# A four-layer graph network on one core: a second message tile and a looser wait in the message phase, and smaller constants

## The reference, cut to what matters

```python
edge_index = jnp.stack([src, dst])
x = x + gin(h, edge_index, ...)                       # two sums of x[src] by dst
x = x + attention(h, edge_attr3_2x32, src, dst, ...)  # below
x = x + tent(h, edge_attr_2, weight, edge_index)      # 4 x 4 tent basis
x = x + spline(h, edge_index, edge_attr_3, ...)       # STN, then a spline convolution

# attention, per edge (two heads of 32 features):
alpha = ee / jnp.maximum(denom[dst], 1e-09)
msg = jax.nn.softmax(en * r_feat * alpha, axis=-1)
g_agg = jax.ops.segment_sum(msg, dst, num_segments=n)

# spline_conv, second one of the STN (64 features in, 64 out):
z = jnp.einsum('ni,kio->nko', x, W).reshape(N * K, Fout)
gathered = z[col[:, None] * K + idx]          # 8 corners of the cell of the edge
msg = jnp.einsum('es,eso->eo', basis, gathered)
out = jax.ops.segment_sum(msg, row, num_segments=N)   # row = src
```

## Time and profile before

| | |
|---|---|
| median of 3 runs | 11980.05 us (11966.1 to 11993.72) |
| span of the profiled execution | 11729.7 us |
| its own time | not given apart from the span |
| TensorE busy, matmul / weight load | 6194.3 us (53%) / 4754.9 us (41%) |
| VectorE busy | 6868.2 us (59%) |
| ScalarE busy | 2989.3 us (25%) |
| GpSimd busy | 7301.5 us (62%) |
| bytes moved | 1760.69 MB, mean 150 GB/s |

### The profile page before, as it was taken

The page is one execution under the profiler, slowest core; times in us unless marked ns, Lnnn a source line. Parts: engine busy times, 40 slices in busy tenths (PEclk is TensorE's granted clock), DMA queues, the critical chain, the costliest instruction groups (busy, mean ns, idle before and its releaser), DMA issues. The chain is left out here.

```text
span 11729.7 us, 173426 instructions
## 1 busy us (share of the span) xinstructions
PE 6194.3 (53%) x40278; PEld 4754.9 (41%) x40279; DVE 6868.2 (59%) x17651; ACT 2989.3 (25%) x7270; POOL 7301.5 (62%) x10729
## 2 busy tenths in 40 slices
PE   4333244444688987666664555555544444662332
PEld 3222244434344443355553555555523333332222
DVE  6555666664322222577787666666656767655555
ACT  0000022221233332111112555555531111220000
POOL 3888788882366665577773333333327877228887
PEclk8555555555688987566665555555565555685555
DMA  6332222224455554222325777777621111587777
GB/s 195 113 113 57 62 62 62 63 62 131 149 190 187 193 186 134 52 74 74 78 77 147 281 285 278 280 284 281 235 81 43 44 41 43 178 323 219 221 222 199
DMA packets 894930, 1760.69 MB, mean 150 GB/s; under 512 B 487010, under 2 KB 487319, under 8 KB 889928
## 3 DMA queue, kind: packets, MB, share of 16 engines
q0 software_dynamic: 317952, 1023.05, 28.3%
q1 hardware_dynamic: 537672, 598.27, 15.2%
q10 hardware_dynamic: 39168, 138.04, 3.0%
HBM read 1150.36 MB, written 611.50 MB: 150 GB/s over the span
## 5 line engine op out<-in xcount | busy, mean ns | idle before, releaser
L1560 POOL DMA_INDIRECT got<-corners,now x1664 | 1679.5, 1009 | 1926.6 <-DVE now L1548 1171.3
L1560 POOL DMA_INDIRECT got<-node_rows,now x1664 | 1639.6, 985 | 1267.3 <-issue 1251.5
L1451 PE MATMUL made_p<-weights,turned 128*128 128x320 bf16 (+4 forms) x7595 | 1541.8, 334 | 203.0 <-ACT z L1417 106.6
L150 POOL MEMSET spare<- 128x192 f32 x4944 | 1376.4, 278 | 3.1
L2342 PE MATMUL sum_p<-msg_s,hot_s 128*128 128x64 f32 x3328 | 734.2, 422 | 931.6 <-DVE msg_s L1824 931.6
L1560 POOL DMA_INDIRECT got<-patches,now x832 | 839.3, 1009 | 565.4 <-DVE now L1548 283.0
L2342 PEld LDWEIGHTS sum_p<-msg_s,hot_s 128*128 128x128 f32 x3328 | 717.7, 332 | 937.5 <-issue 937.5
L1451 PEld LDWEIGHTS made_p<-weights,turned 128*128 128x128 bf16 (+1 forms) x7595 | 657.9, 101 | 1039.0 <-issue 517.0
L896 POOL DMA_INDIRECT d_rows<-row x832 | 942.9, 1133 | 184.3 <-issue 160.1
L1417 ACT COPY z<-made_p 128x384 f32<-128x384 f32 (+3 forms) x1495 | 714.6, 515 | 932.3 <-PE made_p L1451 612.1
L656 POOL DMA_INDIRECT s_rows<-row_now,pos_i x784 | 848.1, 1082 | 155.2 <-issue 136.5
(11 more groups left out here) (411 smaller groups left out, 13596.3 us busy)
## 6 DMA issues: line engine op xcount, KB each, us to landing
corners<-z SPq DMA_DIRECT2D x245, 960.0 KB
corners<-z SPq DMA_DIRECT2D x98, 864.0 KB
d_rows<-empty ACTq DMA_DIRECT2D x32, 1586.0 KB
row<-d_rows SPq DMA_DIRECT2D x104, 488.0 KB
corners<-z SPq DMA_DIRECT2D x49, 672.0 KB
s_rows<-empty ACTq DMA_DIRECT2D x32, 962.0 KB
row<-s_rows SPq DMA_DIRECT2D x104, 296.0 KB
got<-node_rows,now POOLq DMA_INDIRECT x1664
```

The lines of the kernel that those rows point to most:

```text
L150: pool.memset(self.of[:, t, :], 0.0).then_inc(self.cleared, 1)
L1451: m = nc.tensor.matmul(self.made_p[s % banks][:, 0:w], self.turned[b][0:rows, stack, :], weight[0:rows, at:at + w], start=n == 0, stop=n = ...
L1560: pool.indirect_dma_start(out=to[b][:, t, :], out_offset=None, in_=table, in_offset=bass.IndirectOffsetOnAxis(ap=indices.now[b][:, t:t + 1 ...
```

## The change

`msg_s` becomes two tiles used by turns, and the wait at the top of VectorE's iteration asks for one group less. `zero16` shrinks to 128 x 128 and is read four times over by a zero stride (`mid` adds a broadcast dimension) wherever 512 columns are streamed. `before16` is no longer a constant; `place_phase` makes it for itself from the column numbers and the lane number.

```diff
-    k.before16 = sb(k, None, "before16", [LO, LO], BF16)
-    k.zero16 = sb(k, None, "zero16", [LO, 512], BF16)
+    k.zero16 = sb(k, None, "zero16", [LO, LO], BF16)
...
-                dve.tensor_scalar(k.ident16[:], diff[:], 0.0, None, ALU.is_equal)
-                c.after(dve.tensor_scalar(k.before16[:], diff[:], 0.0, None, ALU.is_gt))
+                c.after(dve.tensor_scalar(k.ident16[:], diff[:], 0.0, None, ALU.is_equal))
... place_phase
+        before16 = sb(k, ph, "before16", [LO, LO], BF16)
...
+                dve.tensor_scalar(before16[:], k.column[:], k.lane[:], None, ALU.is_gt)
                 c.after(dve.memset(empty[:], 0.0))
...
+def zeros(k):
+
+    return mid(k.zero16[:], 4)
+
 def clear_sums(k, acc_p, banks):
     for n in range(banks):
-        m = k.nc.tensor.matmul(acc_p[:, n, :], k.zero16[:, 0:LO], k.zero16[:], start=True, stop=False)
+        m = k.nc.tensor.matmul(acc_p[:, n, :], k.zero16[:], zeros(k), start=True, stop=False)
     return m
... message_phase
-        msg_s = sb(k, ph, "msg_s", [LO, 2, T, C])
+        msg_s = [sb(k, ph, "msg_s", [LO, 2, T, C]) for _ in range(2)]
...
-                                m = nc.tensor.matmul(sum_p[b2][:, t, :], hot_s[b2][:, t, :], msg_s[:, n, t, :], start=n == 0, stop=n == 1)
+                                m = nc.tensor.matmul(sum_p[b2][:, t, :], hot_s[b2][:, t, :], msg_s[b2][:, n, t, :], start=n == 0, stop=n == 1)
...
-                        dve.wait_ge(summed_s, g + 1)
+                        dve.wait_ge(summed_s, g)
                         gathered.wait(dve, b2, i * 2 + (b // 2 + 1))
-                        corners.halves(dve, c, got[b2], weight[:, b * T:b * T + T, :], msg_s).then_inc(based_s, 1)
+                        corners.halves(dve, c, got[b2], weight[:, b * T:b * T + T, :], msg_s[b2]).then_inc(based_s, 1)
```

More of the change, by code:

```diff
@@ L461, in _ @@
             def _(pe):
-                nc.tensor.matmul(count_p[:], k.zero16[:, 0:LO], k.zero16[:], start=True, stop=False).then_inc(counted, 1)
+                nc.tensor.matmul(count_p[:], k.zero16[:], zeros(k), start=True, stop=False).then_inc(counted, 1)
                 with pe.Fori(0, pairs) as i:
@@ L469, in _ @@
                         m.then_inc(counted, 1)
-                nc.tensor.matmul(count_p[:], k.zero16[:, 0:LO], k.zero16[:], start=False, stop=True).then_inc(counted, 1)
+                nc.tensor.matmul(count_p[:], k.zero16[:], zeros(k), start=False, stop=True).then_inc(counted, 1)
 def starts_phase(k, s, lists):
@@ L592, in _ @@
                             to = rank_p[b][0:P, t // 4, (t % 4) * 2 * KEYS:(t % 4 + 1) * 2 * KEYS]
-                            nc.tensor.matmul(to, k.before16[:], one[:, t, :], start=True, stop=t == 0)
+                            nc.tensor.matmul(to, before16[:], one[:, t, :], start=True, stop=t == 0)
                             for u in range(t):
@@ L757, in close_sums @@
     for n in range(banks):
-        m = k.nc.tensor.matmul(acc_p[:, n, :], k.zero16[:, 0:LO], k.zero16[:], start=False, stop=True)
+        m = k.nc.tensor.matmul(acc_p[:, n, :], k.zero16[:], zeros(k), start=False, stop=True)
     return m
@@ L843, in _ @@
                 for n in range(2):
-                    m = nc.tensor.matmul(sum_p[1][:, n, :], k.zero16[:, 0:LO], k.zero16[:], start=True, stop=True)
+                    m = nc.tensor.matmul(sum_p[1][:, n, :], k.zero16[:], zeros(k), start=True, stop=True)
                 m.then_inc(summed, 1)
@@ L1651, in _ @@
             def _(pe):
-                nc.tensor.matmul(sum_p[1][:].rearrange("p t f -> p (t f)"), k.zero16[:, 0:LO], k.zero16[:],
+                nc.tensor.matmul(sum_p[1][:].rearrange("p t f -> p (t f)"), k.zero16[:], zeros(k),
                                  start=True, stop=True).then_inc(summed, 1)
@@ L2110, in _ @@
                 for n in range(4):
-                    m = nc.tensor.matmul(spread_p[:, n].rearrange("p a l -> p (a l)"), k.zero16[:, 0:LO], k.zero16[:], start=True, stop=True)
+                    m = nc.tensor.matmul(spread_p[:, n].rearrange("p a l -> p (a l)"), k.zero16[:], zeros(k), start=True, stop=True)
                 m.then_inc(spread, 1)
-                nc.tensor.matmul(top_p[:], k.zero16[:, 0:LO], k.zero16[:], start=True, stop=True).then_inc(summed, 1)
+                nc.tensor.matmul(top_p[:], k.zero16[:], zeros(k), start=True, stop=True).then_inc(summed, 1)
                 pe.sem_inc(started, 1)
```

## The result

The changed kernel took 11627.15 us (median of 4 runs, 11619.72 to 11637.47), beside 11986.88 us for the kernel before on the same chip (4 runs, 11966.1 to 11995.87). The ratio is 0.9683, 95% interval [0.9651, 0.9716]: 360 us faster. The prediction was 11612, range 11550 to 11770.

A forecast was written before the change was run, and what follows sets the result against it. The prediction took VectorE's wait for TensorE's late node-sum increment to bound the message phase. A group falls from 20.47 to 16.9 us, times 103 is 368 us, other parts nothing: 11980 - 368 = 11612 us, range 11550 to 11770.

The forecast's parts named there:

- VectorE's wait: Before the corner multiply: 4.14 us a group waiting for TensorE's node-sum increment, to go entirely, 427 us at most.
- rival C: Before the corner multiply: the wait was for the gather after all, so nothing changes, 11980 us; chance 0.04.
- VectorE's own work, 16.33 us a group: Message phase: the 20.47 us group less 4.14 us idle, the lower bound on a group after the change.
- The loop over two groups, 33.4 us: Message phase: increment, ScalarE's hot_d and exponentials, softmax, corner sums and hand-over, 31.75 plus 1.63 us per two groups.
- the 1.63 us: In the two-group loop: stretch of GpSimd's gather issues beside the corner sums, assumed to delay the increment equally.
- The 12.4: Message phase: microseconds from the node-sum matmuls' start until TensorE's increment arrives, carried as measured, cause unseen.
- Positions 0 and 1, 34.1 us: First two groups of each four: VectorE's work of 15.24 + 18.86 us, more than the two-group loop.
- the 250 us between span and median: Profiled span of 11729.7 us against the 11980.05 median; gains in the span taken off the median one for one.
- The constants and the tile: Smaller zero16: nothing, -1 to +13 us; moved before16: 0 within 1 us; changed tile addresses: 0 within 10 us.
- Rival A: Message phase: corner sums keep GpSimd from issuing gathers; 18.2 to 18.4 us a group, 11767 us; chance 0.12.
- Rival B: Message phase: DMA engines bound it at 300 GB/s, 19.2 us a group, 11849 us; chance 0.09.
- Rival D: Message phase: increments slip behind the next gather burst, 28.7 us after the start; 24.0 us a group, 12344 us; chance 0.05.

The follow-up runs named there:

- exps_first: Changed kernel with ScalarE taking a group's exponentials before making hot_d of the next group; 11561.71 us, ratio 0.9649.
- exps_and_split: Changed kernel with exponentials before the next hot_d and half the cell arithmetic moved from second to first group of four; 11529.05 us, or 10700.6 on a chip without hold.
- before: The kernel before the change, unaltered, in its first trace; 11986.88 us in the first measurement.
- before_again: The kernel before, unaltered, run again for a second trace on another chip; 10748.26 us.

## Why the prediction came out right, and where it did not

*VectorE's wait.* Right in kind and in place: the 4.14 us a group were a wait for TensorE's increment, not for the gather that the view named. With one group more of slack the 426.9 us fell to 11.4, under the 60 asked for; rival C is dead.

*VectorE's own work, 16.33 us a group.* Confirmed closely: where nothing else holds it, on either kind of chip, a group takes 16.36 or 16.37 us.

*The loop over two groups, 33.4 us.* It exists, as `exps_first` shows by removing it, and is mis-sized by 1 us: positions 2 and 3 together take 32.4. The term at fault is the 1.63 us. The prediction had the increment come as long after the last issue as before, but it does not follow the last issue (10.7 or 12.3 us, the same 12.7): the hold grew from 12.4 to 12.67 us, by 0.3. With 0.3 in place of the 1.63 us the sum would be 32.0. The 12.4 itself was read from one group and called that of all normal ones; at position 0 the trace of before has 14 of 26 groups between 8.8 and 11.7 us.

*Positions 0 and 1, 34.1 us.* The term that was missed. They take 37.2. The prediction took VectorE's time at position 1 from one group, in which no control instruction was slow. In 12 of the 26 turns of that same trace some were, and in the changed kernel 24 of 26 turns have them, in the same place behind the corner sums. In the kernel before VectorE waited there anyway for the late count, so they cost next to nothing (positions 1 of 21.3 us with them, 21.2 without); the change took that wait away and uncovered them. The mechanism was in the trace of before and was not looked for; why it became more frequent (the groups stand closer, the DMA share is 0.86 and not 0.74) is not shown. The two errors make (3.1 - 1.0) / 4 = 0.5 us a group, 17.41 for 16.9, 53 us.

*From the phase to the time.* By groups the change gives (20.47 - 17.41) x 103 = 315 us, and the phase itself is 316 shorter (2172.0 and 1856.2); the time fell by 360. The prediction took the 250 us between span and median as lying around the span. It does not (1.7 us here): the profiled execution of the kernel before was itself that much faster than the timed ones. Its other phases show it: second sums 1568 us, scores 1488 and tent 1390, against 1633, 1580 and 1447 in the changed kernel's trace and 1646 to 1671, 1526 to 1595 and 1417 to 1435 in the three later traces of this kind, though no edit touches their loops. With everything but the message phase as long as in the changed kernel's trace (11627.4 - 1856.2 = 9771 us), the timed 11987 us would leave about 2214 for it, 358 more than after. That is an estimate; no trace of such an execution is there. So 11612 lay within 15 us of 11627 by luck: the phase was 53 us too optimistic, and the basis hid some 45 us of gain. The mechanism was right, the two errors of size cancelled.

*The constants and the tile.* Nothing, within 10 us, on a chip without the hold; on the others neither is shown apart from the looser wait. There the fall of the idle time from 426.9 to 11.4 us carries the argument.

*Rival A.* The stretch is real but small: an issue takes 1056 ns in the mean instead of 969, 0.7 us for the eight of a group. GpSimd is slowed beside L1822 and not kept out: in the changed kernel's trace 209 issues overlap the multiply and take 1.29 us in the median (0.93 to 1.99), and the 61 that run beside the additions of the corner sums take 0.94. The Trainium skill ("SBUF — State Buffer", section "SBUF: two separate sides") says less than the prediction drew from it. It keeps GpSimd from writing descriptors while VectorE runs in a 2-port perf mode, and of an instruction with two SBUF inputs it says that it locks the pair only against a GpSimd operation that reads SBUF. The multiply and the additions both have two SBUF inputs, and only beside the multiply does an issue take longer, by at most 1.1 us, about one multiply of 1.2 us; so the second does not tell the two apart. Whether L1822 runs in such a mode, and whether an issue reads SBUF, no run shows.

*Rival B.* The DMA share is 0.86 at 327 GB/s, and `exps_and_split` moves 352 GB/s at 16.37 us a group, so 300 was no ceiling. *Rival D.* The increments kept their place: a median hold of 12.67 us, far from the 28.7 of that rival. Two slips in the working change nothing: the hold from which D decides is 21.7 us (40.9 less 19.2), and the chances that the range leaves out add up to 0.18 to 0.22.

## What to carry to other kernels

Look for the time between an engine's last instruction and the moment others act on its count, and give that wait one more buffer where the engine is not otherwise bound: here it brought 39 us where the count was prompt and 360 us where it was late. A duration read in one group of a loop is not yet that of all groups: idle time called "issue" which grows in some of them is a cost that a denser schedule can multiply. And measure on more than one chip: the same change was worth 3% on one and 0.4% on another.

## What was not expected of the hardware

Three chips ran the kernel before in about 10750 us (10750.4 in 21 runs, 10747.43 in one, 10751.52 in 9). In two other measurements, on one chip or two, it took about 11980 (11986.88 in 4 runs, 11973.92 in 11). In these, TensorE's increment for a 7.06 us burst of matmuls counts after 12.4 to 12.7 us and some of VectorE's register and semaphore instructions take 0.71 us instead of 0.09 or less, both in a stretch in which GpSimd issues gathers and their rows arrive. Other engines have them too: SyncE has 43 register instructions of 0.7 us in the message phase of `before` and none in that of `before_again`. On the three chips the same burst counts after 7.21 us beside the same issues. The granted clock is 0.50 (1.2 GHz) in the message phase on both kinds:

```profile
5905.00:7640.00 1735.00, 1114.76 (x5806) 1099.22 (x5807) 1420.37 (x3115) 1243.10 (x3708) 889.60 (x816) 0.50 0.90 340
```

(the window of the message phase of `before_again`).

The traces of the two kinds differ in one thing more. For the same kernel and the same 173426 instructions the first trace has 93995 records of semaphore updates and `before_again` 153966; in the message phase VectorE's count for `msg_d` is recorded 45 times in the one and 104 times in the other. So the held kind also loses records, and whether the recording of the trace takes part in the hold is not shown. What makes a chip one or the other, what ran beside the kernel there, and whether the gathers' issue or their traffic causes the hold, no run here tells.
